# Mixed tokens of 26 tiles kept in fp32, split into fp16 halves in front of the pairs

## The chip, the cores and the metric
The kernel runs on one core of one Trainium2 chip. The metric is the device time of one execution in microseconds (us), as the median of the runs. The TensorE (PE) of this core was granted 0.989 of its full clock on average, and its full clock from 60 us on.

## The reference, cut to what matters
The input `x` has 64 batches of 64 channels of 1024 values, 4096 rows of length 1024. Two layers each add their result to `x`:

```python
# layer 0
y  = grouped_conv9(x) + ctx + bias
x1 = x + int8_product(y, W0)              # both sides rounded to int8 per row
# layer 1
x2 = einsum('boi,bih->boh', agg_w, x1) + agg_b      # the "mix"; the result is "mixed tokens"
H  = x2 @ W.T + b                          # 1024 x 1024, in fp32 accuracy
z  = x2 @ A                                # low rank, 32 columns
logits = 0.5 * H[:, anchors, :8] / max|.| + 0.5 * (z[:, anchors] @ LiMEs.T) / max|.|
p_mix  = gate(softmax(logits)) @ LiMEs
out = x1 + H + (z * p_mix) @ Bmat * scale
```

The gate needs all of `z` and the first 8 columns of `H`, so it can start only when every tile has been mixed.

## The kernel before, in words
The rows are 32 tiles of 128 (`NT = 32`). Engines work in order, each on its own list of instructions, and meet at named semaphores.

**The loop.** Turn `c` (3 to 31) of the loop on each engine does, for different tiles, the convolution of tile c (`conv`, L462, 16 fp32 calls: 8 on a column half of the array, 8 on a quarter), the mix of tile c-3 (`mix`, L505), the int8 product of tile c-2 (`int_product`, L521), some tiny transposes for row maxima (L528, L532), a transpose of the rounded tokens (`tokens_out`, L493), and in odd turns from 5 on the low rank product of the pair of tiles c-5 and c-4 (`rank_pair`, L552 and L555). After `conv` in turn c the VectorE (DVE) adds the bias (`conv_bias`, L1245), takes row maxima (L1251), the tile's scale (`tile_scale`, L1287), and evicts the two halves of the int8 product (`layer0`, L1277). `conv` itself waits, in front of its third group, for the second `layer0` of the turn before (`f_ready`).

**The mixed tile in fp16 halves.** ScalarE (ACT) reads the mixed tile from PSUM, scales it by a power of two (`t_up`) and writes the high fp16 half to a slot of the ring (`high`, L856, two instructions of 128x512). VectorE subtracts that from the PSUM value and writes the low half (`low`, L1293, two instructions of 128x512). A slot of 128 x 1024 fp32 words holds both halves. `high` waits for `t_up`.

**The low rank product.** For two tiles (256 moving columns) it multiplies the high halves with the high and low parts of the weights (104 columns, 8 matmuls, L552) and the low halves with the high weights (40 columns, alternately in the lower and the upper column half of the array, 8 matmuls, L555). `rank_out` (L1304, L1306) adds the halves for each of the two tiles.

**Two kinds of tiles.** The last six tiles (`RING = 6`, `KEPT = 26`) stay in the ring and are multiplied with W directly (`dense`, L584, 24 matmuls for each half of the columns) while the gate is computed. The 26 others go to DRAM (`save_x2`) and come back (`fetch_x2`) as 13 pairs. Each pair needs 7 products instead of 8 half-size blocks (a scheme of Strassen and Winograd; `pair`, L770, 7 x 12 matmuls of 512 columns). Its left sides are the two tiles and four sums of their halves. ACT brings both tiles to the pair's common scale (`normalized`, L902, one instruction of 128x2048 fp16 for each tile), GpSimd (POOL) adds high and low half to fp32 (`x_sums`, L1119), makes the four sums (`s_sums`, L1128), and ACT and POOL split these into fp16 halves (`s_high` L914, `s_low` L1134). The products read the tiles from the ring and the sums from homes of their own. SyncE issues the fetches in a written order; ACT issues the stores of finished tiles between its own instructions.

Of the kernel before, what the change touches and what calls it, by code (L numbers as in the profile page):

```python
# [15 lines left out]
P = 128  # L16
# [11 lines left out]
ZR = R + E  # L28
# [25 lines left out]
def program(nc, x, x_phases, conv_taps, pack, w_nat, w_rows, w_q, mix_w, w_b, b_ffn, out):  # L54
    ctx = ExitStack()
    with ctx:
# [19 lines left out]
        ring_flat = ring[:, :, :].rearrange("p s l -> p (s l)")  # L76
        x2_cols = ring_flat.bitcast(F16).rearrange("p (s h c t) -> p s h c t", s=RING, h=2, c=NL)
# [52 lines left out]
        z_w = sb("z_w", [P, NL, ZW], F16)  # L130
        z_col = sb("z_col", [P, 1], F32)
# [25 lines left out]
        z_lo = sb("z_lo", [ZR, P], F32)  # L157
# [13 lines left out]
        ratio = sb("ratio", [P, KEPT], F32)  # L171
# [66 lines left out]
        def x_sum(i):  # L238
            return (bias_b, wsum_b)[i]
# [13 lines left out]
        def _(sp):  # L253
# [55 lines left out]
            def save_x2(t):  # L309
                wait(sp, "lo_ready", 2 * t + 2)  # L310
                sp.dma_start(x2_dram[t], ring[:, t % RING, :]).then_inc(sem(f"x2_moved{t % RING}"), 16)
# [45 lines left out]
            def fetch_x2(n):  # L357
                t = ORDER[n]
                if n < 2 * RING:
                    sp.wait_ge(sem("dense_ready"), 2 * (n - RING) + 2)  # L360
                else:
                    sp.wait_ge(sem("prod_ready"), 7 * ((n - 2 * RING) // 2 + 1))
# [56 lines left out]
        def _(pe):  # L419
# [76 lines left out]
            def mix(t):  # L496
# [3 lines left out]
                wait(pe, "lo_ready", 2 * t)  # L500
# [41 lines left out]
            def rank_pair(t):  # L542
                wait(pe, "lo_ready", 2 * t + 4)
                wait(pe, "z_ready", t)
                if t == 0:
                    pe.wait_ge(sem("z_col_ready"), 1)
                if t >= NT - 4:
# [21 lines left out]
            def dense(n, h, lo=0, hi=NL):  # L569
                if lo == 0:  # L570
# [8 lines left out]
                    pe.wait_ge(sem("lo_ready"), 2 * (KEPT + n) + 2)  # L579
# [175 lines left out]
            def x2_part(n, half):  # L755
                return lambda a, k: x2_cols[:, x2_slot(n), a, 4 * half + k, :]
# [16 lines left out]
            def pair(j, deltas):  # L773
                n1, n2 = RING + 2 * j, RING + 2 * j + 1
                sum_a, sum_b, sum_c = pair_banks(j)
                pe.wait_ge(sem("norm_ready"), 2 * j + 2)
# [3 lines left out]
                product(sum_a, x2_part(n1, 0), w_part_of(0, 0), True)  # L780
# [23 lines left out]
                product(sum_c, x2_part(n1, 1), w_part_of(1, 0), True)  # L804
# [3 lines left out]
                product(sum_a, x2_part(n2, 1), t_part(1, 0), False)  # L808
# [9 lines left out]
        def _(act):  # L818
# [78 lines left out]
            def normalized(n):  # L897
                t, s = ORDER[n], x2_slot(n)
                act.wait_ge(sem(f"x2_moved{s}"), 16 * (len(range(s, KEPT, RING)) + n // RING))
                act.wait_ge(sem("ratio_ready"), 1)  # L900
                cols = x2_cols[:, s, :, :, :].rearrange("p h c t -> p (h c t)")
                A(cols, cols, ACT.Copy, scale=ratio[:, t:t + 1]).then_inc(sem("norm_ready"), 1)  # L902

            def s_high(j):
# [7 lines left out]
                for i in (1, 0):  # L912
                    act.wait_ge(sem("s_sum_ready"), 6 * j + (4 if i else 6))
                    A(s_home(j, i)[:, :, 0, :], x_sum(i)[:, :].rearrange("p (s n) -> p s n", s=2), ACT.Copy).then_inc(sem("s_hi_ready"), 1)  # L914
# [45 lines left out]
            A(z_w[:, :, R:ZR], pk[:, PACK["w8"]].rearrange("p (k r) -> p k r", k=NL), ACT.Copy, scale=s_up[:, 0:1]).then_inc(sem("rank_hi_ready"), 1)  # L960

# [47 lines left out]
            A(gateT, bank(2)[:, 0:P], ACT.Copy).then_inc(sem("gateT_ready"), 1)  # L1009
            t_high(3)  # L1010
# [17 lines left out]
            normalized(9)  # L1028
            z_high(1, 0)
# [4 lines left out]
            normalized(11)  # L1034
            store(2)
# [5 lines left out]
            for j in range(1, PAIRS):  # L1041
# [3 lines left out]
                if j + 2 < PAIRS:  # L1045
                    normalized(2 * j + 10)
                    normalized(2 * j + 11)
                store(2 * j + 5)
# [9 lines left out]
        def _(pool):  # L1058
# [52 lines left out]
            def x_sums(j):  # L1111
                for i in range(2):
                    n = RING + 2 * j + i
# [537 lines left out]
```

## Time and profile before
| | before |
|---|---|
| median of 3 runs | 648.18 us (647.95 to 648.85) |
| span of the profiled execution | 646.6 us |
| PE busy | 623.8 us, 96% |
| DVE / ACT / POOL busy | 418.3 / 335.3 / 336.2 us |
| mean DMA rate | 214 GB/s |

The span is counted from the first to the last instruction. The whole time of the profiled execution itself is not given beside it; the three timed runs lie 1.4 to 2.3 us above the span. The page draws a busy PE nearly everywhere; VectorE is at 7 to 8 tenths in the first half and at 4 in the second.

### The profile page before, as it was taken

How to read it: one execution, taken by the hardware profiler on the slowest of the kernel's cores; microseconds unless marked ns; L12 is line 12 of the kernel's file. 1: busy time of each engine (PE TensorE's matmuls, PEld its weight loads, DVE VectorE, ACT ScalarE, POOL GpSimd, SP SyncE). 2: the span in 40 equal slices, each digit the busy share in tenths (PEclk: the TensorE clock that was granted, in tenths of full speed). 3: DMA queues.
4: the chain of work that ended last, by engine and by line, in shares of the span. 5: the costliest groups of instructions: out<-in, count | busy, mean ns of one | idle time of the engine just before them, and what ended most of it. 6: DMA issues, size and time to landing. Idle time of an engine off the chain costs nothing.

```text
span 646.6 us, 14948 instructions
## 1 busy us (share of the span) xinstructions
PE 623.8 (96%) x5865; PEld 337.3 (52%) x5898; DVE 418.3 (65%) x891; ACT 335.3 (52%) x566; POOL 336.2 (52%) x223
## 2 busy tenths in 40 slices
PE   7789999999999999999999999999999999999997
PEld 5556565566566666656554444444444444444443
DVE  5958778877787778787537797745544433444434
ACT  2857898667778777776652436334333313333100
POOL 3012222217778522225485689886866678666400
PEclk8799999999999999999999999999999999999999
DMA  8969877677799797764529014554555433457103
GB/s 299 361 137 365 295 284 273 233 266 276 280 342 336 285 359 280 259 229 140 217 73 357 35 34 153 206 203 156 196 195 193 158 132 136 162 197 259 66 1 130
DMA packets 46707, 138.38 MB, mean 214 GB/s; under 512 B 13180, under 2 KB 13468, under 8 KB 46465
## 3 DMA queue, kind: packets, MB, share of 16 engines
q1 hardware_dynamic: 41886, 120.65, 52.6%
q10 hardware_dynamic: 4752, 16.78, 6.4%
q8 instruction: 47, 0.77, 0.5%
q14 instruction: 22, 0.18, 0.1%
HBM read 89.13 MB, written 48.28 MB: 213 GB/s over the span
## 4 chain that ended last, share of the span: by engine, by line
PE 51%; DVE 1%; issue 0%; ACT 0%; DVEq 0%
PE ps L770 36%; PE ps L584 9%; PE ps L752 2%; PE ps L521 2%; PE ps L505 1%; PE ps L462 0%; PE ps L552 0%; DVE z_lo L1304 0%; DVE unscale L1441 0%; DVE ring L1293 0%; DVE yb L1245 0%; DVE zT L1306 0%; PE ps L555 0%; PE ps L730 0%; PE ps L493 0%
## 5 line engine op out<-in xcount | busy, mean ns | idle before, releaser
L1088 POOL TENSOR_TENSOR x<-x_in,f_both 128x512 f32<-128x512 f32 x64 | 74.0, 1157 | 195.9 <-DVE f_both L1277 195.9
L521 PE MATMUL ps<-wqT,yq_both 128*128 128x512 bf16 x479 | 113.2, 379 | 6.0 <-issue 4.6
L462 PE MATMUL ps<-x_ph,conv_w 64*64 64x256 f32 (+1 forms) x1024 | 98.2, 396 | 2.2 <-DMA conv_w<-in_conv_taps 2.0
L863 ACT ACTIVATE yv<-yb,yinv 128x128 f32<-128x128 f32 x256 | 78.0, 389 | 2.3 <-DVE yinv L1268 2.2
L902 ACT ACTIVATE ring<-ring,ratio 128x2048 f16<-128x2048 f16 x26 | 50.6, 1994 | 51.1 <-DVE wst L1537 14.1
L770 PE MATMUL ps<-ffn_wT,ring 128*128 128x512 f16 x312 | 71.6, 379 | 0.0
L462 PEld LDWEIGHTS ps<-x_ph,conv_w 64*64 64x64 f32 (+1 forms) x1024 | 51.1, 137 | 37.4 <-issue 14.2
L521 PEld LDWEIGHTS ps<-wqT,yq_both 128*128 128x128 bf16 x512 | 45.2, 97 | 48.4 <-issue 1.0
L1245 DVE TENSOR_TENSOR yb<-ps,ybias 128x1024 f32<-128x1024 f32 x32 | 39.1, 1223 | 41.1 <-PE ps L462 41.0
L584 PE MATMUL ps<-ffn_wT,ring 128*128 128x512 f16 x288 | 64.6, 379 | 0.0
L856 ACT ACTIVATE ring<-ps,t_up 128x512 f16<-128x512 f32 x64 | 40.5, 683 | 45.5 <-issue 38.1
L1119 POOL TENSOR_TENSOR bias_b<-ring 128x1024 f32<-128x1024 f16 x13 | 27.8, 2137 | 48.4 <-ACT ring L902 48.2
L1550 DVE SCALAR_TENSOR_TENSOR x_in<-ps,unscale,x_in 128x512 f32<-128x512 f32 x30 | 22.5, 750 | 43.7 <-PE ps L770 43.5
L1277 DVE SCALAR_TENSOR_TENSOR f_both<-ps,tok_scale,wsc_b 128x512 f16<-128x512 f32 x64 | 47.8, 748 | 4.1 <-PE ps L521 3.3
L770 PEld LDWEIGHTS ps<-ffn_wT,ring 128*128 128x128 f16 x312 | 30.5, 98 | 36.8
L846 ACT ACTIVATE yq_both<-ps 128x1024 bf16<-128x1024 f16 x32 | 32.7, 1023 | 31.3 <-PE ps L493 31.0
L1293 DVE SCALAR_TENSOR_TENSOR ring<-ps,t_up,ring 128x512 f16<-128x512 f32 x64 | 46.9, 737 | 0.8 <-ACT ring L856 0.8
L584 PEld LDWEIGHTS ps<-ffn_wT,ring 128*128 128x128 f16 x288 | 27.2, 98 | 32.1 <-issue 0.8
L1550 DVE SCALAR_TENSOR_TENSOR wst<-ps,unscale,wst 128x512 f32<-128x512 f32 x28 | 21.0, 750 | 35.2 <-PE ps L770 35.1
L1251 DVE TENSOR_REDUCE rowmax<-yb 128x8 f32<-128x1024 f32 x32 | 39.0, 1220 | 1.0
L505 PEld LDWEIGHTS ps<-mixT,x 64*64 64x64 f32 x2048 | 35.8, 135 | 5.2 <-issue 1.6
L1550 DVE SCALAR_TENSOR_TENSOR x<-ps,unscale,x 128x512 f32<-128x512 f32 x21 | 15.8, 750 | 31.1 <-PE ps L770 31.1
(284 smaller groups left out, 1096.6 us busy)
## 6 DMA issues: line engine op xcount, KB each, us to landing
x_ph<-in_x_phases SPq DMA_DIRECT2D x32, 516.0 KB, 6.1
x_in<-in_x SPq DMA_DIRECT2D x32, 512.0 KB, 6.4
x_scratch<-x SPq DMA_DIRECT2D x32, 512.0 KB, 2.8
x_scratch<-ring SPq DMA_DIRECT2D x26, 512.0 KB, 4.1
ring<-x_scratch SPq DMA_DIRECT2D x26, 512.0 KB, 4.3
wst<-in_w_rows SPq DMA_DIRECT2D x12, 512.0 KB, 5.0
x_in<-x_scratch SPq DMA_DIRECT2D x12, 512.0 KB, 6.5
out<-x_in ACTq DMA_DIRECT2D x12, 512.0 KB, 3.6
```

Source lines behind the costliest of these rows:

```text
L462: return mm(ps_conv[o, g * 2 * MB:(g + 1) * 2 * MB], conv_w[k, g, w.start + o.start:w.start + o.stop], xp[k, g, :, view], start=first, sto ...
L505: last = mm(bank(2 + e)[j * 64:(j + 1) * 64, k * CH:(k + 1) * CH], x1[b, t % 2, l:l + 64], mixT[b, t, b], start=True, stop=True)
L521: last = mm(acc_bank(t, h), yqT[:, t % 2, p, :], wqT[:, p, h * HALF:(h + 1) * HALF], start=p == 0, stop=p == PH - 1)
L584: last = mm(o, x2_cols[:, x2_slot(n), a, k, :], ffn_wT[:, w, k, h * HALF:(h + 1) * HALF], start=k == 0 and i == 0, stop=k == NL - 1 and i ...
L770: last = mm(b, left(a, k), right(w, k), start=fresh and k == 0 and i == 0, stop=k == 3 and i == 2, skip_group_check=True)
L856: A(x2_cols[:, t % RING, 0, :, h * CH:(h + 1) * CH], bank(2 + h).rearrange("p (c t) -> p c t", c=NL), ACT.Copy, scale=t_up[:, t % 4:t % 4 ...
L863: last = A(yv[:, s, :], yb[:, t % 2, s, :], ACT.Copy, scale=yinv[:, s:s + 1], bias=MAGIC)
L902: A(cols, cols, ACT.Copy, scale=ratio[:, t:t + 1]).then_inc(sem("norm_ready"), 1)
L1088: g.tensor_tensor(x1[:, t % 2, s], x_in[:, t % 3, s], f16[:, s], ALU.add).then_inc(sem("x1_ready"), 1)
L1277: v.scalar_tensor_tensor(f16[:, s], acc_bank(t, h), tok_scale[:, t % 4:t % 4 + 1], wsc_b[:, s], ALU.mult, ALU.mult).then_inc(sem("f_ready" ...
L1293: v.scalar_tensor_tensor(x2_cols[:, t % RING, 1, :, cols], bank(2 + h).rearrange("p (k t) -> p k t", k=NL), t_up[:, t % 4:t % 4 + 1], x2_c ...
L1550: v.scalar_tensor_tensor(buf, src, unscale[:, t:t + 1], buf, ALU.mult, ALU.add).then_inc(sem("pair_folded"), 1)
```

## The change
For the 26 tiles that become pairs, `high` copies the mixed tile from PSUM to the ring in fp32, without a scale and without waiting for `t_up`, and `low` does nothing. The low rank product of these tiles takes fp32 operands: 8 calls of 40 weight columns, alternately in the lower and upper column half. `rank_out` is then two additions for the pair, without scales. In front of the pairs, `normalized` scales 1024 fp32 values, `x_high` (ACT) and `x_low` (POOL) write the fp16 halves of the parts of the two tiles that the products read (the whole of the first tile, the second half of the second) to one of three homes, and `s_sums` then works in place in the ring slot. `x_sums` is gone. The first product of a pair now waits for `x_low` where it waited for `normalized`; `mix` waits for `high` where it waited for `low`; the fetch of later tiles waits for `s_low` of the pair that used the slot, where it waited for all of that pair's products.

```diff
             def rank_pair(t):
-                wait(pe, "lo_ready", 2 * t + 4)
+                if t < KEPT:
+                    pe.wait_ge(sem("hi_ready"), 2 * t + 4)
...
+                if t < KEPT:
+                    for k in range(NL):
+                        o = 64 * (k % 2)
+                        last = mm(rank[o:o + ZR, 0:2 * P], z_f[:, k, :], x2_sums[:, s:s + 2, k, :],
+                                  start=k < 2, stop=k >= NL - 2, skip_group_check=True)
+                    last.then_inc(sem("z_psum"), 1)
+                    return
...
             def high(t, h):
...
-                    wait(act, "t_ready", 2 * t + 2)
+                    if t >= KEPT:
+                        act.wait_ge(sem("t_ready"), 2 * t + 2)
...
+                if t < KEPT:
+                    A(x2_sums[:, t % RING, :, h * CH:(h + 1) * CH], bank(2 + h).rearrange("p (c t) -> p c t", c=NL),
+                      ACT.Copy).then_inc(sem("hi_ready"), 1)
+                    return
...
             def normalized(n):
...
-                cols = x2_cols[:, s, :, :, :].rearrange("p h c t -> p (h c t)")
-                A(cols, cols, ACT.Copy, scale=ratio[:, t:t + 1]).then_inc(sem("norm_ready"), 1)
+                A(ring[:, s, :], ring[:, s, :], ACT.Copy, scale=pair_inv[:, t:t + 1]).then_inc(sem("norm_ready"), 1)
+
+            def x_high(j):
+                act.wait_ge(sem("norm_ready"), 2 * j + 2)
...
+                if j >= 3:
+                    act.wait_ge(sem("prod_ready"), 7 * (j - 2))
+                for i, lo in ((1, HALF), (0, 0)):
+                    A(x_home(j, i)[:, 0, lo:L], x_tile(j, i)[:, lo:L], ACT.Copy).then_inc(sem("x_hi_ready"), 1)
...
+            def x_low(j):
+                for i, lo in ((1, HALF), (0, 0)):
+                    pool.wait_ge(sem("x_hi_ready"), 2 * j + (1 if i else 2))
+                    h = x_home(j, i)
+                    g.tensor_tensor(h[:, 1, lo:L], x_tile(j, i)[:, lo:L], h[:, 0, lo:L], ALU.subtract).then_inc(sem("x_lo_ready"), 1)
...
             def low(t, h):
+                if t < KEPT:
+                    return
...
             def rank_out(t):
+                if t < KEPT:
+                    dve.wait_ge(sem("z_psum"), t // 2 + 1)
+                    dve.wait_ge(sem("z_bias_ready"), t // 8 + 1)
+                    cols = slice(t * P, (t + 2) * P)
+                    link(v.tensor_tensor(z_lo[:, :], rank_bank(t)[64:ZW, 0:2 * P], zT[64:ZW, cols], ALU.add))
+                    v.tensor_tensor(zT[0:ZR, cols], rank_bank(t)[0:ZR, 0:2 * P], z_lo[:, :], ALU.add).then_inc(sem("z_ready"), 2)
+                    return
```

Besides, two ACT instructions write the fp32 weights `z_f` once in front of the loop, the tile `ratio` goes, and the program is built with a smaller scratch area for descriptors made by software (2048 bytes); all of its large transfers use the hardware queues.

## Rows read from the trace of the kernel before
**Rows 1.** Windows: us, busy us of each engine (x instructions), clock, DMA share, GB/s.
```profile
240.00:300.00 60.00, 58.88 (x888) 36.70 (x892) 48.42 (x121) 41.94 (x93) 18.94 (x16) 1.00 0.70 247
450.00:500.00 50.00, 50.00 (x233) 22.64 (x232) 23.85 (x32) 17.32 (x12) 36.50 (x22) 1.00 0.50 184
```
**Rows 2.** Timeline of PE, 200 to 219 us: start, length, instructions.
```profile
200.92 0.62 PE L493 MATMUL ps<-identh,yv 128*128 128x128 f16 x8
201.38 1.04 PE L552 MATMUL ps<-ring,z_w 128*104 128x256 f16 x8
202.34 0.62 PE L555 MATMUL ps<-ring,z_w 128*40 128x256 f16 x8
202.79 2.92 PE L462 MATMUL ps<-x_ph,conv_w 128*64 128x256 f32 x32
205.54 1.11 PE L505 MATMUL ps<-mixT,x 64*64 64x64 f32 x64
210.27 0.22 PE L532 MATMUL ps<-ident,chanmax_rep 8*128 8x8 f32 x1
210.43 0.62 PE L493 MATMUL ps<-identh,yv 128*128 128x128 f16 x8
210.98 2.98 PE L462 MATMUL ps<-x_ph,conv_w 128*64 128x256 f32 x32
213.78 1.11 PE L505 MATMUL ps<-mixT,x 64*64 64x64 f32 x64
```
**Rows 3.** Groups by form, PE alone, 204.50 to 204.70 us: busy us, mean ns.
```profile
L462 PE MATMUL ps<-x_ph,conv_w 64*64 64x256 f32 x4 | 0.4, 427 | 0.0
L462 PE MATMUL ps<-x_ph,conv_w 128*64 128x256 f32 x2 | 0.4, 378 | 0.0
```
**Rows 4.** Groups by form, whole span: busy us, mean ns, idle before.
```profile
L1293 DVE SCALAR_TENSOR_TENSOR ring<-ps,t_up,ring 128x512 f16<-128x512 f32 x64 | 46.9, 737 | 0.8 <-ACT ring L856 0.8
L884 ACT ACTIVATE wst<-wst,w_up 128x1024 f32<-128x1024 f32 x4 | 4.5, 1138 | 0.2 <-DMA wst<-in_w_rows 0.2
L914 ACT ACTIVATE f_both<-wsum_b 128x1024 f16<-128x1024 f32 x7 | 7.4, 1057 | 35.2 <-POOL wsum_b L1128 35.2
L1134 POOL TENSOR_TENSOR wsc_b<-wsum_b,wsc_b 128x1024 f16<-128x1024 f32 x6 | 12.8, 2128 | 0.0
```
**Rows 5.** Timeline of PE, 66 to 124 us; in brackets idle before and its end.
```profile
68.59 0.18 PE L485 MATMUL ps<-x1sum,ones_b 128*128 128x1 bf16 x1 [0.37 <-ACT f_both L841]
77.46 0.81 PE L521 MATMUL ps<-wqT,yq_both 128*128 128x512 bf16 x3 [0.16 <-issue]
78.11 0.17 PE L485 MATMUL ps<-x1sum,ones_b 128*128 128x1 bf16 x1
81.63 3.31 PE L462 MATMUL ps<-x_ph,conv_w 128*64 128x256 f32 x32
103.78 0.81 PE L521 MATMUL ps<-wqT,yq_both 128*128 128x512 bf16 x3 [0.16 <-issue]
105.59 0.18 PE L485 MATMUL ps<-x1sum,ones_b 128*128 128x1 bf16 x1 [0.99 <-ACT f_both L841]
118.32 0.22 PE L532 MATMUL ps<-ident,chanmax_rep 8*128 8x8 f32 x1 [0.15 <-DVE chanmax_rep L1257]
119.03 3.19 PE L462 MATMUL ps<-x_ph,conv_w 128*64 128x256 f32 x32
```
**Rows 6.** Timelines of ACT (96 to 124 us) and DVE (72 to 86 us).
```profile
97.66 1.27 ACT L856 ACTIVATE ring<-ps,t_up 128x512 f16<-128x512 f32 x2 [1.28 <-DVE t_down L1288]
...
82.02 0.75 DVE L1277 SCALAR_TENSOR_TENSOR f_both<-ps,tok_scale,wsc_b 128x512 f16<-128x512 f32 x1
```
**Rows 7.** Timelines of POOL, 336 to 424 us, and PE, 300 to 400 us.
```profile
365.57 1.26 POOL L1104 TENSOR_TENSOR conv_w<-conv_w 128x512 f32<-128x512 f32 x1
301.77 3.30 PE L462 MATMUL ps<-x_ph,conv_w 128*64 128x256 f32 x32
...
393.17 2.75 PE L770 MATMUL ps<-ffn_wT,ring 128*128 128x512 f16 x12
```

More of the change, by code:

```diff
@@ L130, in program @@
         z_w = sb("z_w", [P, NL, ZW], F16)
+        z_f = sb("z_f", [P, NL, ZR], F32)
+        x_part = sb("x_part", [P, 2, L], F32)
         z_col = sb("z_col", [P, 1], F32)
@@ L236, in t_home, with x_home, x_tile @@
             return t_homes[q].rearrange("p (w r n) -> p w r n", w=2, r=2)
-        def x_sum(i):
-            return (bias_b, wsum_b)[i]
+        x_homes = ((x_part[:, 0, :], x_part[:, 1, :]), tuple(yb[:, i, :, :].rearrange("p n m -> p (n m)") for i in range(2)),
+                   (bias_b[:, :], wsum_b[:, :]))
+        def x_home(j, i):
+            return x_homes[j % 3][i].bitcast(F16).rearrange("p (a n) -> p a n", a=2)
+        def x_tile(j, i):
+            return ring[:, x2_slot(RING + 2 * j + i), :]
         s_homes = ((yq_both[:, :, :].rearrange("p a n -> p (a n)").bitcast(F16), f_both[:, :, :].rearrange("p a n -> p (a n)")),
@@ L499, in mix @@
                 wait(pe, "x1_ready", 2 * t + 2)
-                wait(pe, "lo_ready", 2 * t)
+                if t <= KEPT:
+                    wait(pe, "hi_ready", 2 * t)
+                else:
+                    pe.wait_ge(sem("lo_ready"), 2 * (t - KEPT))
                 for k in range(NL):
@@ L753, in delta, with x2_part @@
                 last.then_inc(sem("delta_ready"), 1)
-            def x2_part(n, half):
-                return lambda a, k: x2_cols[:, x2_slot(n), a, 4 * half + k, :]
+            def x2_part(j, i, half):
+                return lambda a, k: x_home(j, i)[:, a, (4 * half + k) * P:(4 * half + k + 1) * P]
             def s_part(j, i, s):
@@ L803, in pair @@
                 wait(pe, "pair_folded", 7 * j)
[L804 removed]
+                product(sum_c, x2_part(j, 0, 1), w_part_of(1, 0), True)
                 for n in deltas[5]:
@@ L807, in pair @@
                 pe.wait_ge(sem("pair_folded"), 7 * j + 5)
-                product(sum_a, x2_part(n2, 1), t_part(1, 0), False)
+                product(sum_a, x2_part(j, 1, 1), t_part(1, 0), False)
             dense(5, 0)
@@ L960, in _ @@
             A(z_w[:, :, R:ZR], pk[:, PACK["w8"]].rearrange("p (k r) -> p k r", k=NL), ACT.Copy, scale=s_up[:, 0:1]).then_inc(sem("rank_hi_ready"), 1)
+            A(z_f[:, :, 0:R], pk[:, PACK["a"]].rearrange("p (k r) -> p k r", k=NL), ACT.Copy, scale=s_up[:, 1:2]).then_inc(sem("z_f_ready"), 1)
+            A(z_f[:, :, R:ZR], pk[:, PACK["w8"]].rearrange("p (k r) -> p k r", k=NL), ACT.Copy, scale=s_up[:, 0:1]).then_inc(sem("z_f_ready"), 1)
             for c in range(3, NT):
@@ L1009, in _ @@
             A(gateT, bank(2)[:, 0:P], ACT.Copy).then_inc(sem("gateT_ready"), 1)
+            x_high(0)
             t_high(3)
@@ L1028, in _ @@
             normalized(9)
+            x_high(1)
             z_high(1, 0)
@@ L1034, in _ @@
             normalized(11)
+            x_high(2)
             store(2)
@@ L1047, in _ @@
                     normalized(2 * j + 11)
+                    x_high(j + 2)
                 store(2 * j + 5)
@@ L1151, in _ @@
             t_sums(3)
-            x_sums(0)
+            x_low(0)
             t_low(3)
@@ L1156, in _ @@
             for j in range(1, PAIRS):
-                x_sums(j)
+                x_low(j)
                 s_sums(j)
```

54 lines of the change are left out of this document (25 added, 29 removed).

## The prediction
> **What bounds the kernel now.** I read the table of windows first. PE is busy for 58.9 of 60 us late in the loop and for 50.0 of 50 in the pairs, at the full clock throughout [rows 1]. So nearly every microsecond that PE's instruction list gains or loses is a microsecond of the time, and what the other engines gain counts only where PE waits for them. A busy figure overlaps pipelined matmuls, so I then took the timeline of PE and measured from start to start. A turn of the loop from one conv to the next is 8.19 us without a low rank product (210.98 less 202.79). The reader is to see two things there: PE goes from one piece to the next without a pause, and the only regular gap is one of 0.16 us behind the mix [rows 2, 5]. Last I looked for turns that are longer than their kind, since there another engine bounds: there are six that matter, all listed below.
>
> **PE: the low rank product.** Before: from the first L552 to the conv behind it, 202.79 - 201.38 = 1.41 us [rows 2]. After: 8 calls in fp32. What such a call costs, conv shows: its 16 calls make 32 instructions, so a call is two, and the first 16 of them (the 8 calls on a column half, 256 columns, all 128 rows, the same shape as the new ones) run from 202.79 to about 204.50, where the first quarter-array instruction stands beside the last half-array ones [rows 2, 3]. That is 1.71 us for 8 calls with both halves at work. The new product has 8 calls of that shape, with 40 weight columns where conv has 64: 1.71 us. There is one more item: the eight transposes in front take 201.38 - 200.92 = 0.46 us when the low rank product follows on the whole array, and 210.98 - 210.43 = 0.55 us when conv follows on column halves [rows 2]; the new product begins on a half, so it pays 0.09. Behind it comes conv, on halves already, as it did behind L555, so nothing changes there. A pair of tiles costs 1.71 + 0.09 - 1.41 = 0.39 us more. All 13 pairs of the kept tiles stand in the loop (turns 5 to 29); the pairs 26, 28 and 30 keep the old form. 13 x 0.39 = 5.1 us. Bounds: 4.6 if the 0.09 does not show and the weight loads of 40 columns help a little, 6.2 if the alternation costs another 0.08 each time.
>
> The Trainium skill (FP8 and Floating Point Precision, on true FP32) says that such a product is four passes through the array; this trace agrees, with two instructions of two passes each. It is the rule that speaks against the change: 8 calls x 4 passes on half the array are 16 full passes of 256 columns, where the fp16 form had 8 full and 8 half ones, 12. By the rule alone the pair would cost a third more than 1.28 us, 0.43, and 13 pairs 5.5. TensorEngine Tiling, Key Properties (Trainium skill) says that changing the tiling mode drains the array; the 0.09 above would be that drain, and the two rows agree.
>
> **VectorE and ACT in the loop.** `low` goes for 26 tiles: 52 x 737 ns = 38 us of VectorE [rows 4]. PE bounds the loop, so most of this buys nothing. Two waits move earlier, though. (a) The second `layer0` of a turn stands behind the first `low`, so its result comes 0.73 us earlier, and conv's third group waits for it. In turn 7 that `layer0` ends at 82.02 + 0.75 = 82.77, while conv began at 81.63 and wants it about 0.85 later (half of the half-array stage of 1.71); this conv lasts 3.31 us instead of 2.98 [rows 2, 5, 6]. (b) ACT's `high` no longer waits for `t_up`. In turn 8 ACT stood idle for 1.28 us in front of `high`, which began at 97.66 [rows 6]; two extra copies behind it then made everything late, and in turn 9 the row total on PE came 105.59 - 103.78 = 1.81 us behind the int8 product instead of 78.11 - 77.46 = 0.65 [rows 5].
> What this gives back, turn by turn: turn 5, the row total waited with 0.37 us idle [rows 5] and 0.15 more hidden under the matmul in front, 0.5; turn 7, 0.33; turn 9, 1.81 - 0.65 = 1.16; turn 10, where VectorE was late with the channel maxima (0.15 idle [rows 5], the rest hidden), 0.4; turn 11, conv 3.19 us instead of 2.98 [rows 2, 5] and a wait of 0.18 for a scale, 0.4; turn 31, conv 3.30 us [rows 7], 0.3. Together 3.1. Then there is a trifle that repeats: conv takes 2.80 us behind transposes (213.78 - 210.98) but 2.75 behind a low rank product (205.54 - 202.79) [rows 2], where `layer0` had been done long before. If that 0.05 is the same wait, it goes in 9 turns, 0.4. I take half of it: 3.3 us back. Bounds 0 (the waits are replaced by others of equal length) and 4.0.
> `high` writing fp32 costs what it did: ACT's 1024-element copies take 1138 ns to fp32 and 1057 to fp16 [rows 4], under 0.1 us an instruction, and ACT has time to spare in each turn. Bound: 0 to 0.3 us in all. The two writes of `z_f` stand behind ACT's third rounding of tokens, in front of the first row sums; estimated from the two like them that are there, under 1 us of ACT, and PE reads these sums later than that: 0 to 0.5 us, taken as 0. `rank_out` becomes two instructions of twice the width instead of four, off the path.
>
> **The pairs.** PE's 7 x 12 matmuls and the deltas are unchanged and leave no gap, so only lateness can cost. ACT for a pair: before 2 x 1994 ns of `normalized`; after 2 x 1138 and 1057 + about 600 for `x_high`, 3.9 us against 4.0 [rows 4]. POOL: before 2.1 + 2.3 us of `x_sums`; after 2128 ns and about 1270 for half of it [rows 4], 1.0 us less. The new condition is that the first product waits for `x_low`. For pair 0: POOL is through with the sums in front of it at 366.8, `x_high` is done before, so `x_low` ends at about 370.2; PE wants it at 393.2 [rows 7]. Cover 23 us. Later pairs are prepared two ahead, 38 us of PE work, against some 20 us of ACT and POOL. The fetches wait for something earlier than before, so SyncE's queue does not hold them longer. Cost 0; bound, if the cover went, a few tenths for each pair.
>
> **The sum.** The profiled span is 646.6 us; what lies around it (1.6 to the median of 648.18) does not change. 648.2 + 5.1 - 3.3 = 650.0 us. Without the return it is 653.3.
>
> **Rivals.**
> 1. *The pass cost stands alone* (the waits in turns 5 to 11 only change hands: ACT and VectorE are in order, and the two copies and the delta weights are still there). For it: VectorE had unexplained pauses in turn 7. Against: the idle of ACT in front of `high` is plain. 653.3 us. Chance 0.2.
> 2. *Not slower*: the PE step that turns the maxima back (L532) waits for VectorE in every turn. It begins at 210.27 and the transposes 0.16 later [rows 2], where the product in front of it should be through 0.1 us earlier. If a VectorE with 1.5 us less work in a turn brings the maxima sooner, 26 turns give 2.6 us more: 647.4. Against: the maxima hang on conv, bias and `layer0`, none of which stands behind `low` in that chain. It decides if those maxima come 0.1 us earlier. Chance 0.13.
> 3. *The halves don't run together in fp32 at 40 columns*: 16 instructions of 0.213 us in a row, 3.4 us, 13 x 1.7 = 22 us more, about 672. Against: conv does it. Chance 0.04.
> 4. *The pairs wait*, through `x_low` or the homes that are reused three pairs later: say 0.5 us for each, 13 x 0.5 = 6.5, 656.5. Chance 0.05.
>
> **How the numbers follow.** The forecast, 650.0, has 0.58; its own range is 648.8 to 651.6. The whole range is 647.5 to 653.8: it takes in rivals 1 and 2 and leaves out 3, 4 and a little. What a measurement of this kernel can tell from no change is 0.2%, 1.3 us, so "within" is 646.9 to 649.5. The forecast's case is slower by over that with about 0.65 of its weight, rivals 1, 3, 4 wholly; rival 2 is mostly within. Faster by over 0.2% is left 0.06.
>
> **What would show it.** L552 and L555 are left in three pairs only; 16 fp32 instructions for each of 13 pairs in 1.7 us, and 0.55 us of transposes in front of them. A turn with a low rank product longer by 0.39, one without unchanged or 0.05 shorter. The row total of turn 9 at 0.65 behind the product, conv at 2.75 to 2.8 us in turns 7, 10 and 31. PE without a gap from the first pair on. The prediction is wrong if the fp32 product takes another time than 1.7 us, if the excess of turns 5 to 11 stays, or if any pair begins late.

## The result and the profile after

The change makes the kernel slower: 650.71 us (median of 5 runs, 650.49 to 651.80) against 648.18 us (647.53 to 648.85), ratio 1.0044 [1.0031, 1.0056]. The profiled execution has a span of 649.7 us where the one of before had 646.6.

The busy figures say that all other engines lost work. This is the first part of the page of the kernel after:

```profile
PE 634.5 (98%) x5898; PEld 336.7 (52%) x5898; DVE 374.7 (58%) x812; ACT 327.6 (50%) x594; POOL 322.2 (50%) x223
```

VectorE lost 43.6 us of work, ACT 8 and POOL 14, and PE is drawn busy for 98% of the span where it was 96% (mostly records that the trace of before lacks, see below). The windows late in the loop and in the pairs (us, busy us of each engine in the order PE, PEld, DVE, ACT, POOL, clock, DMA share, GB/s) answer to [rows 1]:

```profile
240.00:300.00 60.00, 60.00 (x861) 35.51 (x861) 37.91 (x100) 41.99 (x97) 17.42 (x15) 1.00 0.70 249
450.00:500.00 50.00, 50.00 (x233) 22.64 (x232) 23.13 (x31) 15.54 (x16) 34.50 (x22) 1.00 0.48 167
```

PE is full in both, at its full clock (2.4 GHz). In the pairs it runs the same 233 instructions as before, so the pairs give and take nothing. In the loop VectorE went from 48.4 to 37.9 us of 60, and PE has no free time that this could give back. The timeline of PE after, 200 to 224 us (start, length, instructions), beside [rows 2]:

```profile
201.65 0.62 PE L501 MATMUL ps<-identh,yv 128*128 128x128 f16 x8
202.20 1.93 PE L569 MATMUL ps<-ring,z_f 128*40 128x256 f32 x16
203.96 2.93 PE L470 MATMUL ps<-x_ph,conv_w 128*64 128x256 f32 x32
206.71 1.11 PE L516 MATMUL ps<-mixT,x 64*64 64x64 f32 x64
...
211.60 0.62 PE L501 MATMUL ps<-identh,yv 128*128 128x128 f16 x8
212.15 2.98 PE L470 MATMUL ps<-x_ph,conv_w 128*64 128x256 f32 x32
214.95 1.11 PE L516 MATMUL ps<-mixT,x 64*64 64x64 f32 x64
```

From start to start: the transposes 0.55 us in front of the new product as in front of conv (they were 0.46 in front of the old one), the new product 203.96 - 202.20 = 1.76 us where the old one took 1.41. The turn without a product is still 8.19 us (212.15 - 203.96), conv behind the transposes still 2.80.

All turns of the loop, from the start of one conv to the start of the next, in us:

| turn | before | after | after less before | given back (0.43 less that, in turns with a product) |
|---|---|---|---|---|
| 5 | 10.11 | 10.00 | -0.11 | 0.54 |
| 7 | 9.90 | 10.00 | +0.10 | 0.33 |
| 9 | 10.73 | 10.00 | -0.73 | 1.16 |
| 10 | 8.58 | 8.19 | -0.39 | 0.39 (no product) |
| 11 | 10.25 | 10.44 | +0.19 | 0.24 |
| 13 | 10.18 | 10.57 | +0.39 | 0.04 |
| 15 to 25, 29 | 9.90 | 10.33 | +0.43 | 0 |
| 27 | 10.20 | 10.64 | +0.44 | 0 |
| 4, 6, 8, 12 to 30 even | 8.18 to 8.76 | the same to 0.01 | 0 | 0 |
| 31 and the dense part | 91.40 | 91.08 | -0.32 | 0.32 (no product) |

(From turn 15 on an odd turn also holds two small products for the gate, so 9.90 is its kind there and 9.57 in turns 5 to 9.) The last line runs from the conv of turn 31 to the first product of a pair (301.77 to 393.17, and 305.12 to 396.20). So 13 x 0.43 = 5.6 us were added and 3.0 were given back: +2.6 us. The measured medians differ by 2.5. The two spans differ by 3.1, and 0.4 of it stands in front of turn 5, where the start of the kernel puts conv at 63.34 or 63.74; in all the profiles taken here conv of turn 4 begins anywhere between 54.15 and 55.70 us, and in the two profiles of this same kernel at 55.43 and 54.93, so the start is scatter.

### The profile page after: what moved, and what is told of

It reads as the page before. It is cut to its first block, busy times and chain, and to the rows that moved or that the text cites. A ratio compares the mean times of both kernels' runs of the same rounds, so it can differ in the third digit from the quotient of the medians.

```text
span 649.7 us, 14865 instructions
## 1 busy us (share of the span) xinstructions
PE 634.5 (98%) x5898; PEld 336.7 (52%) x5898; DVE 374.7 (58%) x812; ACT 327.6 (50%) x594; POOL 322.2 (50%) x223
## 4 chain that ended last, share of the span: by engine, by line
PE 79%; DVE 1%; issue 0%; ACT 0%; DVEq 0%
PE ps L792 36%; PE ps L532 12%; PE ps L606 9%; PE ps L470 9%; PE ps L516 3%; PE ps L569 3%; PE ps L774 2%; PE ps L501 2%; PE ps L589 1%; PE ps L543 0%; PE ps L539 0%; PE ps L574 0%; DVE unscale L1487 0%; DVE z_lo L1351 0%; DVE ring L1333 0%
## 5 line engine op out<-in xcount | busy, mean ns | idle before, releaser
L532 PE MATMUL ps<-wqT,yq_both 128*128 128x512 bf16 x512 | 120.5, 379 | 0.8 <-ACT wsc_b L849 0.8
L470 PE MATMUL ps<-x_ph,conv_w 64*64 64x256 f32 (+1 forms) x1024 | 96.6, 390 | 0.0
L532 PEld LDWEIGHTS ps<-wqT,yq_both 128*128 128x128 bf16 x512 | 45.2, 97 | 48.2 <-issue 0.9
L1166 POOL TENSOR_TENSOR ring<-ring 128x512 f32<-128x512 f32 x52 | 66.0, 1268 | 4.0
L606 PE MATMUL ps<-ffn_wT,ring 128*128 128x512 f16 x288 | 64.6, 379 | 0.0
L927 ACT ACTIVATE ring<-ring,pair_inv 128x1024 f32<-128x1024 f32 x26 | 28.4, 1140 | 54.4 <-DVE x_ph L1583 14.4
L606 PEld LDWEIGHTS ps<-ffn_wT,ring 128*128 128x128 f16 x288 | 27.2, 98 | 32.1 <-issue 0.8
L516 PE MATMUL ps<-mixT,x 64*64 64x64 f32 x2048 | 35.6, 218 | 0.0
L862 ACT ACTIVATE f_both<-x 128x1024 bf16<-128x1024 f32 x32 | 33.4, 1043 | 0.0
L879 ACT ACTIVATE ring<-ps 128x512 f32<-128x512 f32 x52 | 27.8, 585 | 2.6 <-PE ps L516 2.3
L792 PE MATMUL ps<-ffn_wT,x_part 128*128 128x512 f16 x120 | 27.5, 379 | 0.0
```

Of the source, the lines that this page charges most:

```text
L470: return mm(ps_conv[o, g * 2 * MB:(g + 1) * 2 * MB], conv_w[k, g, w.start + o.start:w.start + o.stop], xp[k, g, :, view], start=first, sto ...
L516: last = mm(bank(2 + e)[j * 64:(j + 1) * 64, k * CH:(k + 1) * CH], x1[b, t % 2, l:l + 64], mixT[b, t, b], start=True, stop=True)
L532: last = mm(acc_bank(t, h), yqT[:, t % 2, p, :], wqT[:, p, h * HALF:(h + 1) * HALF], start=p == 0, stop=p == PH - 1)
L606: last = mm(o, x2_cols[:, x2_slot(n), a, k, :], ffn_wT[:, w, k, h * HALF:(h + 1) * HALF], start=k == 0 and i == 0, stop=k == NL - 1 and i ...
L792: last = mm(b, left(a, k), right(w, k), start=fresh and k == 0 and i == 0, stop=k == 3 and i == 2, skip_group_check=True)
L1166: g.tensor_tensor(o, x, y, op).then_inc(sem("s_sum_ready"), 1)
```

## The experiments

Each run is compared with the kernel before on the same chip; what matters more is its difference from the kernel after, for which there is a second measurement at the end: 650.67 us. The turn lengths are taken from the trace as above.

### The price of the product: the product twice

```diff
-                    for k in range(NL):
+                    for k in list(range(NL)) + list(range(NL)):
                         o = 64 * (k % 2)
                         last = mm(rank[o:o + ZR, 0:2 * P], z_f[:, k, :], x2_sums[:, s:s + 2, k, :],
```

> The changed kernel with the fp32 low rank product of each of the 13 pairs done twice over, the second time on top of the first from the start. Theory A (PE bounds the loop and a product costs its 16 instructions at 0.107 us, 1.71 to 1.76 us): 13 x 1.71 = 22.2 us more, 672.9. Rival B (part of the product lies under waits): clearly less than 22 us more.

Measured: 673.15 us (672.66 to 674.36), ratio 1.0382 [1.0364, 1.0400], so 22.4 us above the kernel after. PE in this kernel, 212 to 219 us:

```profile
213.03 3.65 PE L569 MATMUL ps<-ring,z_f 128*40 128x256 f32 x32
216.51 2.93 PE L470 MATMUL ps<-x_ph,conv_w 128*64 128x256 f32 x32
```

32 instructions take 216.51 - 213.03 = 3.48 us, twice 1.76 less the 0.04 that the second pass saves at its start; 13 x 1.72 = 22.4, all of what was measured. It follows that each microsecond of this product counts in full: nothing lies beside it. What the old product cost (1.41 us, and 0.09 less in the transposes) was not doubled; it is read from the trace, but the 0.43 us between the two stands in the length of seven turns in which PE's list differs in nothing else, 9.90 against 10.33 us. The 0.04 is worth a second look: the product costs 1.76 us behind the transposes and 1.72 behind work on halves.

### Does the alternation of the column halves matter

```diff
-                    for k in range(NL):
+                    for n, k in enumerate((0, 2, 4, 6, 1, 3, 5, 7)):
                         o = 64 * (k % 2)
```

(The four calls on the lower half first, then the four on the upper; the same calls.)

> The changed kernel with the 8 calls of the low rank product ordered by column half, four for the lower and then four for the upper, instead of alternating. Theory A (the price of 1.76 us needs both halves at work at once; instructions on one half run one after another): 16 x 0.213 = 3.4 us a pair, 13 x 1.65 = 21.5 us more, 672. Rival B (the array takes 0.107 us for such an instruction anyway): no change, 650.7.

Measured: 663.04 us (662.47 to 663.60, 2 runs), ratio 1.0220 [1.0198, 1.0242]: 12.3 us above the kernel after. PE, 109 to 116 us:

```profile
109.56 2.17 PE L569 MATMUL ps<-ring,z_f 128*40 128x256 f32 x13
111.36 0.43 PE L470 MATMUL ps<-x_ph,conv_w 128*64 128x256 f32 x1
111.57 0.38 PE L569 MATMUL ps<-ring,z_f 128*40 128x256 f32 x1
...
112.00 0.38 PE L569 MATMUL ps<-ring,z_f 128*40 128x256 f32 x1
112.06 3.08 PE L470 MATMUL ps<-x_ph,conv_w 128*64 128x256 f32 x29
114.96 1.11 PE L516 MATMUL ps<-mixT,x 64*64 64x64 f32 x64
```

The product is not over when conv begins at 111.36: the last instructions of its upper half alternate with the first ones of conv on the lower half. Nor are its own halves one behind the other. The first row below is a piece of PE's timeline from the start of the upper half on; then come windows of 0.1 us with this product alone (busy of PE, instructions in the window), then the same in the kernel after, and the product's last two instructions there:

```profile
110.46 0.63 PE L569 MATMUL ps<-ring,z_f 128*40 128x256 f32 x3
```

```profile
110.30:110.40 0.10, 0.10 (x2) 0.05 (x1) 1.00 0.80 328
110.90:111.00 0.10, 0.10 (x4) 0.10 (x2) 1.00 0.80 328
```

```profile
202.90:203.00 0.10, 0.10 (x4) 0.10 (x2) 1.00 0.92 369
...
203.74 0.39 PE L569 MATMUL ps<-ring,z_f 128*40 128x256 f32 x2
```

At first two instructions are in flight, those of the lower half; from 110.46 on there are four, as in the alternating product (the row does not name the half; that the new ones are the upper half's is read from the starts, 0.21 to 0.22 us apart on a half), though three of the eight instructions of the lower half are still to start (13 of the 16 have started when conv begins). So the upper half starts 0.90 us late and ends as much late. The turn with the product grows by 0.04 us and the turn that this conv opens from 8.19 to 9.04, together 0.89 x 13 = 11.6 of the 12.3 us. The forecast for a serial product (some 21.5 us) is missed because the upper half starts while the lower one is still at work. What conv does on the free lower half gains nothing: from the last start of the product (112.00) to the mix (114.96) it is 2.96 us, in the kernel after from 203.74 to 206.71 it is 2.97. So the two halves do run together in fp32 with 40 columns, and it is the alternation that gets this from the first instruction on.

### ACT waits for `t_up` again

```diff
-                    if t >= KEPT:
-                        act.wait_ge(sem("t_ready"), 2 * t + 2)
+                    act.wait_ge(sem("t_ready"), 2 * t + 2)
```

> The changed kernel with one wait put back: ScalarE's first half of `high` waits for the tile's scale in all tiles, as before. Theory A (the waits of turns 5 and 9 in the old kernel came from this wait, and their going gave 0.54 + 1.16 = 1.7 us back): these two turns grow again to 10.5 and 11.1 us from 10.00, span +1.7, about 652.4. Rival B (the row totals are in time now because a turn with the low rank product is 0.43 us longer and leaves slack): both turns stay at 10.0, time as the changed kernel, 650.7.

Measured: 652.33 us (651.88 to 653.00), ratio 1.0061 [1.0046, 1.0076]. Turn 5 is 10.36 us (+0.36 on the kernel after), turn 7 10.10 (+0.10), turn 9 10.98 (+0.98), every other turn as after: +1.44. First ACT in turn 8 of this kernel, then PE's row totals in turns 5 and 9 (in brackets the idle time and what ended it):

```profile
98.52 1.08 ACT L878 ACTIVATE ring<-ps 128x512 f32<-128x512 f32 x2 [2.00 <-DVE t_down L1325]
```

```profile
68.81 0.18 PE L493 MATMUL ps<-x1sum,ones_b 128*128 128x1 bf16 x1 [0.19 <-ACT f_both L862]
106.27 0.18 PE L493 MATMUL ps<-x1sum,ones_b 128*128 128x1 bf16 x1 [0.81 <-ACT f_both L862]
```

In the kernel after, the same copy and the same total:

```profile
95.96 1.06 ACT L879 ACTIVATE ring<-ps 128x512 f32<-128x512 f32 x2
```

```profile
104.84 0.17 PE L493 MATMUL ps<-x1sum,ones_b 128*128 128x1 bf16 x1
```

One wait of ACT that hangs on VectorE brings back the chain of [rows 6]: ACT idle for 2.00 us in front of `high`, the copies behind it late, the row sums late, PE idle for 0.81 us. This one wait is worth 0.36 of the 0.54 us given back in turn 5 and 0.98 of the 1.16 in turn 9, 1.34 of the 3.0 in all. The 0.10 of turn 7 is not a part of them: here it stands in front of the row total, while the 0.33 that turn 7 had before stood inside conv.

### VectorE gets its instruction back

```diff
                 if t < KEPT:
+                    dve.wait_ge(sem("t_ready"), 2 * t + 2)
...
+                    v.scalar_tensor_tensor(junk, bank(2 + h).rearrange("p (k t) -> p k t", k=NL), t_up[:, t % 4:t % 4 + 1],
+                                           x2_sums[:, t % RING, :, cols], ALU.mult, ALU.subtract).then_inc(sem("junk_ready"), 1)
                     return
...
                 if t <= KEPT:
                     wait(pe, "hi_ready", 2 * t)
+                    wait(pe, "junk_ready", 2 * t)
```

(The second place is `mix` on PE. The instruction is of the shape of `low` and writes to `x_part`, which nothing reads before the pairs write it anew.)

> The changed kernel with VectorE's work put back: for each half of the 26 tiles it reads the PSUM bank and the ring slot and writes a 128x512 fp16 result to a spare place, where `low` stood, and the mix waits for it as it did. The extra work is not part of the result. Theory A: the waits that hung on VectorE come back in turns 7, 10, 11 and 31 (0.33 + 0.39 + 0.24 + 0.32 = 1.3 us), about 652.0; conv in turn 7 takes 3.1 instead of 2.80 us. Rival B (VectorE's work was under PE throughout, and its late results were pauses of other cause): no change, 650.7.

Measured: 651.35 us (650.84 to 652.09), ratio 1.0047 [1.0030, 1.0065], 0.6 above the kernel after. Turns 5 to 10 are as after, to 0.02 us, and turn 11 is 10.46; turn 13 is longer by 0.05. Only conv in turn 31 is at 3.31 us, as it was before. Its line on PE and the one on VectorE inside it:

```profile
304.38 3.31 PE L470 MATMUL ps<-x_ph,conv_w 128*64 128x256 f32 x32
```

```profile
304.64 0.20 DVE L1307 RECIPROCAL yinv<-yscale 128x8 f32<-128x8 f32 x1 [0.44 <-issue]
```

38 us of VectorE put back cost 0.07 us in turns 11 and 13, and the intervals of the two kernels overlap. The 0.33 us of turn 31 is not the put-back work: this edit puts nothing into turn 31, whose `low` is that of tile 28, one of the last six, and stands in all these kernels. What is new there is that VectorE stood still for 0.44 us. The theory that VectorE's load made turns 7, 10 and 11 long falls for this kernel.

### Both, and then the third edit too

`both_back` has the two edits above. `all_back` has them and also `rank_out` as four instructions of 128 columns instead of two of 256:

```diff
-                    link(v.tensor_tensor(z_lo[:, :], rank_bank(t)[64:ZW, 0:2 * P], zT[64:ZW, cols], ALU.add))
-                    v.tensor_tensor(zT[0:ZR, cols], rank_bank(t)[0:ZR, 0:2 * P], z_lo[:, :], ALU.add).then_inc(sem("z_ready"), 2)
+                    for i in range(2):
+                        cols = slice((t + i) * P, (t + i + 1) * P)
+                        link(v.tensor_tensor(z_lo[:, 0:P], rank_bank(t)[64:ZW, i * P:(i + 1) * P], zT[64:ZW, cols], ALU.add))
+                        v.tensor_tensor(zT[0:ZR, cols], rank_bank(t)[0:ZR, i * P:(i + 1) * P], z_lo[:, 0:P], ALU.add).then_inc(sem("z_ready"), 1)
```

> Both of these together, so only the low rank product, the writes of the fp32 weights and the pairs differ from the old kernel. Theory A: all 3.0 us of the return are gone; 650.7 + 3.0 = 653.7, which is 648.2 + 13 x 0.43 + about 0.8 for the weights at the start less 0.9 of differences in the start. Rival B: 650.7 to 651.5.

> As `both_back`, and `rank_out` again in four instructions of 128 columns instead of two of 256. Read from the profile only: turn 10, which took 8.58 us in the old kernel and 8.20 with both put back. Theory A2 (in turn 10 of the old kernel VectorE had its share of B and then four instructions of `rank_out` in front of conv's bias; the two wide ones save about 0.7 us there, and the longer product gives PE's side 0.43 us more): the bias starts some 0.3 us late, turn 10 at 8.2 to 8.4. Rival B2 (`rank_out` plays no part): 8.20 exactly as in `both_back`.

Measured: `both_back` 652.96 us (650.70 to 653.25), ratio 1.0062 [1.0041, 1.0083]; `all_back` 653.0 us in its one run. `both_back` has turn 5 at 10.37, 7 at 10.10, 9 at 10.98, 10 at 8.20, 13 at 10.62, and conv of turn 31 at 3.31 us: the turns show the two edits simply added, 1.44 + 0.05 + 0.33 = 1.8 us (the median is 2.2 us above that of the kernel after, among runs that spread over 2.6). Both forecasts are missed: of the 3.0 us given back, some 1.2 did not return. VectorE of `both_back` in turn 31, and then PE:

```profile
305.52 0.73 DVE L1338 SCALAR_TENSOR_TENSOR ring<-ps,t_up,ring 128x512 f16<-128x512 f32 x1
...
306.85 0.20 DVE L1306 RECIPROCAL yinv<-yscale 128x8 f32<-128x8 f32 x1 [0.44 <-issue]
306.98 0.75 DVE L1315 SCALAR_TENSOR_TENSOR f_both<-ps,tok_scale,wsc_b 128x512 f16<-128x512 f32 x1
```

```profile
306.59 3.31 PE L470 MATMUL ps<-x_ph,conv_w 128*64 128x256 f32 x32
```

Here is the price of the pause: VectorE stands still for 0.44 us with nothing to wait for, the second `layer0` behind it ends at 307.73, 1.14 after conv began, and conv, which wants it after about 0.85, loses 0.33. In the kernel before it is the same picture in turn 7, and in turn 31 too:

```profile
81.89 0.20 DVE L1268 RECIPROCAL yinv<-yscale 128x8 f32<-128x8 f32 x1 [0.45 <-issue]
...
302.15 0.75 DVE L1277 SCALAR_TENSOR_TENSOR f_both<-ps,tok_scale,wsc_b 128x512 f16<-128x512 f32 x1 [0.28 <-issue]
```

In the kernel after the one pause falls into turn 29, where it costs nothing. Its turn 31 has the same `low` in front of the second `layer0` as before, and no pause; this `layer0` ends at 305.91, 0.79 us after conv began, just in time, and conv is at 2.98 us as in turn 7:

```profile
295.55 0.75 DVE L1315 SCALAR_TENSOR_TENSOR f_both<-ps,tok_scale,wsc_b 128x512 f16<-128x512 f32 x1 [0.28 <-issue]
...
304.06 0.73 DVE L1333 SCALAR_TENSOR_TENSOR ring<-ps,t_up,ring 128x512 f16<-128x512 f32 x1
...
305.16 0.75 DVE L1315 SCALAR_TENSOR_TENSOR f_both<-ps,tok_scale,wsc_b 128x512 f16<-128x512 f32 x1
```

```profile
81.93 2.98 PE L470 MATMUL ps<-x_ph,conv_w 128*64 128x256 f32 x32
...
305.12 2.98 PE L470 MATMUL ps<-x_ph,conv_w 128*64 128x256 f32 x32
```

So the excess of turns 7 and 31 is this: with `low` in front of it, `layer0` is only just in time, and a pause that falls there costs 0.33 us. In turn 31 the change took nothing away but the pause's place; in turn 7 it took away both, and `low` put back without a pause costs nothing there (`dve_back`, `both_back`). Whether a pause alone would, no run shows. `all_back` has a second way to be late, without a pause: in turn 7 its `low` waits 0.16 us for ACT's `high`, `layer0` ends 1.03 us after conv began, and the turn is 10.22 us.

In `all_back` turn 10 is 8.19 us: the 0.39 us of turn 10 in the kernel before could not be brought back by any of the three edits. What is left of the differences (the old product and the scaled `rank_out`, ACT's slower fp16 copy) was not put back one by one. The cause of turn 10's 0.39 stays open, and so do 0.18 in each of turns 5 and 9 and the 0.24 of turn 11: about 1.0 us of the 3.0. Turn 4 (+0.22) and turn 11 (+0.39) of `all_back` are longer than in the kernel after; the one of turn 11 has such a pause in it too (125.70, 0.25 us).

### The `z_f` writes

```diff
-            A(z_f[:, :, 0:R], pk[:, PACK["a"]].rearrange("p (k r) -> p k r", k=NL), ACT.Copy, scale=s_up[:, 1:2]).then_inc(sem("z_f_ready"), 1)
-            A(z_f[:, :, R:ZR], pk[:, PACK["w8"]].rearrange("p (k r) -> p k r", k=NL), ACT.Copy, scale=s_up[:, 0:1]).then_inc(sem("z_f_ready"), 1)
...
+                if c == 3:
+                    A(z_f[:, :, 0:R], pk[:, PACK["a"]].rearrange("p (k r) -> p k r", k=NL), ACT.Copy, scale=s_up[:, 1:2]).then_inc(sem("z_f_ready"), 1)
+                if c == 4:
+                    A(z_f[:, :, R:ZR], pk[:, PACK["w8"]].rearrange("p (k r) -> p k r", k=NL), ACT.Copy, scale=s_up[:, 0:1]).then_inc(sem("z_f_ready"), 1)
                 tokens_sb(c - 1)
```

> The changed kernel with ScalarE's two writes of the fp32 low rank weights moved from in front of the loop into turns 3 and 4, into the time in which ScalarE waits for the transposes. Theory A (these writes made the first row sums late: in turn 3 the row total stands 1.65 us behind the product in front of it, where 0.87 is usual): turn 3 shorter by 0.8 us, 649.9. Rival B (the row total of turn 3 is late for another reason, the first transfers and the low clock at the start): no change, 650.7.

Measured: 650.86 us (649.15 to 652.76, 10 runs), ratio 1.0040 [1.0025, 1.0054]: no change. But the trace shows why one has to look further than one wait. PE in turn 3, first the kernel after, then this one:

```profile
51.25 0.18 PE L493 MATMUL ps<-x1sum,ones_b 128*128 128x1 bf16 x1 [0.62 <-ACT f_both L862]
...
52.90 0.27 PE L539 MATMUL ps<-ident,rowmax 128*8 128x128 f32 x1
```

```profile
50.46 0.18 PE L493 MATMUL ps<-x1sum,ones_b 128*128 128x1 bf16 x1
...
52.74 0.27 PE L539 MATMUL ps<-ident,rowmax 128*8 128x128 f32 x1 [0.57 <-DVE bound L1321]
```

The row total waited 0.62 us for ACT, and the writes were a cause of it; without them this idle is gone, and 0.57 us appear in front of the next step, which waits for VectorE. Turn 3 is 9.67 us in both. The writes cost nothing because another wait of the same length stands behind theirs.

### The cover of the pairs

```diff
-                    g.tensor_tensor(h[:, 1, lo:L], x_tile(j, i)[:, lo:L], h[:, 0, lo:L], ALU.subtract).then_inc(sem("x_lo_ready"), 1)
+                    for n in range(2):
+                        last = g.tensor_tensor(h[:, 1, lo:L], x_tile(j, i)[:, lo:L], h[:, 0, lo:L], ALU.subtract)
...
+                    last.then_inc(sem("x_lo_ready"), 1)
```

> The changed kernel with GpSimd's `x_low` done twice for each part, about 3.4 us more of GpSimd for each pair. Theory A (the new wait of the pairs' first product has 20 us and more of cover): no change, PE without a gap, 650.7. Rival B (the pairs stand close to GpSimd): up to 13 x 3.4 us more.

Measured: 651.70 us (649.40 to 652.10), ratio 1.0042 [1.0025, 1.0060], the ratio of the kernel after. The window 450 to 500 us:

```profile
450.00:500.00 50.00, 50.00 (x233) 22.61 (x232) 22.93 (x31) 16.51 (x18) 45.48 (x28) 1.00 0.49 175
```

POOL goes from 34.5 to 45.5 us of 50 and PE still does its 233 instructions. In the kernel after `x_low` of the first pair ends 369.83 + 3.25 = 373.08 us, and PE takes it at 396.20 (POOL, then PE):

```profile
369.83 3.25 POOL L1157 TENSOR_TENSOR x_part<-ring,x_part 128x512 f16<-128x512 f32 x2
```

```profile
396.20 2.75 PE L792 MATMUL ps<-ffn_wT,x_part 128*128 128x512 f16 x12
```

### The gains without the price: the kernel before, smoothed

If what the change gave back are late waits in turns 5 to 11 and pauses that meet no slack, the kernel before can have that by order alone, without the fp32 product.

```diff
-                if 4 <= c < 8:
-                    z_bias(c - 4)
-                if c == 8:
+                if c in (5, 11, 12, 14):
+                    z_bias((5, 11, 12, 14).index(c))
+                if c == 13:
                     act.wait_ge(sem("b_loaded"), 16)
...
-                if c == 9:
+                if c == 14:
                     delta_weights()
...
                 low(c - 3, 0)
-                scales(c)
                 layer0(c - 2, 1)
+                scales(c)
                 low(c - 3, 1)
```

`before_smooth2` differs in turn 11 alone, where the order is `scales`, `layer0`, `low`, `low`.

> The old kernel, its arithmetic untouched, with the work of the long turns moved: the four scalings of z's bias from turns 4 to 7 to turns 5, 11, 12 and 14, the two copies of B from turn 8 to 13, VectorE's share of B from turn 9 to 14, and the second `layer0` of a turn in front of the tile scales. Theory A (the waits that the change took away can be had without the fp32 product): turn 5 0.5, turn 7 0.3, turn 9 1.2, turn 10 0.4, turn 31 0.3 us shorter, 2.5 to 3 us less than before, 645.5. Rival B (the late pieces come back in the turns to which they are moved): 648.2.

> As `before_smooth`, but in turn 11 VectorE makes the tile scales ahead of the second `layer0`, since there PE waits for them in front of a transpose (1.46 us in front of it instead of 0.81 in the old kernel). Theory A: turn 11 shorter by 0.6 to 0.9 us, 644.6 us. Rival B (that transpose waits for the running maximum of W's row sums): no change, 645.4.

Measured: 645.36 us (643.99 to 646.75), ratio 0.9948 [0.9927, 0.9968], and 645.10 us (644.70 to 646.43), ratio 0.9946 [0.9928, 0.9964]. Turns 5, 7 and 9 are 9.57, 9.57 and 9.56 us in the first, turn 10 is 8.19. Turn 4 of the second is 8.84 us (8.31 in the first), in a start that scatters. Turn 11 is 10.71, because the first weight bound (L679) now waits for a `scales` that had moved behind; in the second it is 10.04, 0.67 shorter as forecast, of which the median shows 0.26. The line of `before_smooth`, then that of `before_smooth2`:

```profile
126.42 0.27 PE L679 MATMUL ps<-ident,w_max 128*1 128x128 f32 x1 [0.84 <-DVE yinv L1268]
```

```profile
125.52 0.27 PE L679 MATMUL ps<-ident,w_max 128*1 128x128 f32 x1 [0.17 <-DVE yinv L1268]
...
81.53 2.98 PE L462 MATMUL ps<-x_ph,conv_w 128*64 128x256 f32 x32
...
104.00 0.17 PE L485 MATMUL ps<-x1sum,ones_b 128*128 128x1 bf16 x1
```

The row total of turn 9, which had 0.99 us of idle [rows 5], has none, and conv of turn 7 is at 2.98. `before_smooth2` beats both kernels, by 3.2 us the one before and by 5.6 us the one after, and does the same arithmetic as the kernel before. The two moves (ACT's and VectorE's pieces to later turns, `layer0` ahead of the tile scales) were not run apart; 0.66 us of the gain is turns 7 and 31, which also have no pause in front of `layer0` here. The same order in the kernel after wasn't run; its turns 5 to 10 have nothing left to give back.

### The kernel after once more

> The changed kernel again, on the same chip as the kernel before and the smoothed one, for the size of the difference. Theory A (13 x 0.43 = 5.6 us for the product, 2.7 to 3.0 back): 648.2 + 2.6 to 2.9, a ratio of 1.0040 to 1.0045. Rival B (the profiled spans, 3.1 us apart, are the better measure): 1.0048.

Measured: 650.67 us (649.51 to 652.03, 10 runs), ratio 1.0034 [1.0022, 1.0046], 2.4 us. Its median is that of the first measurement to 0.04 us. The ratio lies just below the forecast from the turns (1.0040 to 1.0045), which its interval holds; the 1.0048 of the spans is outside. Its turns without a product are 8.19 us again, though its trace draws a 0.16 us gap in them that the first profile of this kernel did not have (below).

## Why the prediction came out as it did

The forecast was 650.0 us, the result 650.7. The balance is the one that it named, a price on PE of which a part is given back where other engines had been late, and the price is shown. Of the return less than half came for the reason given; that its sum came out nearly right is in part luck. Step by step:

- **PE bounds, and its list is the time.** Right. 22.4 us more in the list made 22.4 us more in the time; 38 us more on VectorE made 0.07 in the turns that have them (0.6 in the median, with the pause of turn 31).
- **The product: 0.39 us for a pair, 5.1 in all.** Right in kind, small in size: this is the mis-sized term. It measured 0.43 and 5.6. The mode change was right to the row (0.55 us of transposes, +0.09, in each of the 13 turns). The 1.71 us, read off inside conv [rows 3], is right for 16 instructions that follow work on halves (1.72 in `rank_twice`); what is missing is 0.04 for the start behind the transposes, where it takes 1.76. The rows had it: conv too takes 2.80 us behind transposes and 2.75 behind a product, and the prediction put that 0.05 down as a wait. The pass count of the Trainium skill (FP8 and Floating Point Precision, on true FP32), which the prediction set beside its own sum as an estimate of 0.43 for a pair and 5.5 in all, comes to the measured 0.43 and 5.6, but not by its own terms: the product alone took 0.35 more (1.76 - 1.41), and the rest is the 0.09 in front.
- **The waits given back: 3.3 us.** 3.0 measured. Turns 5, 7, 9, 10 and 31 gave 0.54, 0.33, 1.16, 0.39 and 0.32, as listed (0.5, 0.33, 1.16, 0.4, 0.3); turn 11 gave 0.24 instead of 0.4. The reason (b), ACT no longer waits for `t_up`, is shown for 1.34 us, in turns 5 and 9. The reason (a), `low` in front of the second `layer0`, is not borne out: in turn 31 `low` stands there in both kernels, and in turn 7 it did nothing when put back. Both turns had a pause of VectorE before. The 0.32 of turn 31 came back because in the kernel after the pause falls elsewhere, the 0.33 of turn 7 for that or because `low` no longer takes the slack, which no run separates. The prediction knew of such pauses (rival 1) but gave them no term. With the pause in turn 31, as in `dve_back`, 0.33 less is given back. Turn 10's 0.39 came as predicted, but not for the reason given: none of the three edits brought it back. Its cause is open, as are 0.18 us in each of turns 5 and 9 and the 0.24 of turn 11.
- **The 0.05 us of conv behind transposes.** Did not go; conv is at 2.80 there as before. It is no wait, so the 0.2 taken for it was wrong. That it has to do with the change from the whole array to halves is likely, as it stands behind transposes alone and the new product pays 0.04 there as well (1.76 against 1.72), but no run took it apart.
- **A regular gap of 0.16 us behind the mix.** There is none. It was a record missing from the trace. The rows of the page for the int8 product, before and after:

```profile
L521 PE MATMUL ps<-wqT,yq_both 128*128 128x512 bf16 x479 | 113.2, 379 | 6.0 <-issue 4.6
```

```profile
L532 PE MATMUL ps<-wqT,yq_both 128*128 128x512 bf16 x512 | 120.5, 379 | 0.8 <-ACT wsc_b L849 0.8
```

  479 of 512 matmuls were recorded before, all 512 after; "idle" falls from 6.0 to 0.8 us and the turn stays at 8.19. The prediction put nothing into its sum for this gap, so it cost nothing but a false picture; the PE share of 96% before and 98% after is largely that.
- **`high` in fp32 at no cost.** Better than that. The three groups, ACT after, ACT before for `high`:

```profile
L879 ACT ACTIVATE ring<-ps 128x512 f32<-128x512 f32 x52 | 27.8, 585 | 2.6 <-PE ps L516 2.3
L927 ACT ACTIVATE ring<-ring,pair_inv 128x1024 f32<-128x1024 f32 x26 | 28.4, 1140 | 54.4 <-DVE x_ph L1583 14.4 <-DVE wst L1583 14.3 <-DVE x_in L1583 13.2
```

```profile
L856 ACT ACTIVATE ring<-ps,t_up 128x512 f16<-128x512 f32 x64 | 40.5, 683 | 45.5 <-issue 38.1 <-DVE t_down L1288 4.3 <-PE ps L505 3.1
```

  585 ns instead of 683. Off the path, it shows nowhere in the time. `normalized` at 1140 ns is the 1138 of [rows 4].
- **`z_f` at no cost.** Right in the sum, for a reason that was not given: PE did wait for ACT there (0.62 us), but a wait of the same length stood behind it.
- **The pairs at no cost.** Right: cover 23.1 us where 23 was predicted, and with `x_low` twice still no gap.

Of the rivals, the first (nothing given back, 653.3) falls with turns 5 to 10, though what it had for it, the pauses, is what made turns 7 and 31 long; the second (L532 sooner in every turn, 647.4) with the 8.19 us that did not move; the third (the halves do not run together) with 1.76 us for 16 instructions; the fourth with the windows of the pairs.

## What to carry to other kernels

When PE is full, price a change by the start-to-start time of PE's pieces alone: 38 us of VectorE's work were worth almost nothing, 0.43 us in each of 13 turns of PE's own list cost 5.6. Turns that are longer than their kind are where other engines count; look there for a wait that can be moved by order alone, before paying for it with arithmetic, since that gave 3.2 us without the price. Before an instruction is blamed for such a turn, look whether it is still there in the kernel that is faster: turn 31 kept its `low` and got shorter all the same. And test an edit that removes a wait by the length of the turn, not by the idle in front of one instruction: the next wait may already stand behind it.

## What the runs showed of the hardware

- An fp32 product with 128 rows, 40 weight columns and 256 moving columns takes 0.110 us for an instruction (1.76 / 16), with instructions alternating between column halves, and 0.107 (1.72 / 16) behind other work on halves. Grouped by half, the first instruction of the second half starts 0.90 us in, beside the last four of the first half, and the loss is 0.89 us for a product.
- Behind 50 us, VectorE stands still for 0.25 to 0.45 us with nothing that it waits for: twice in the profile of before, not at all in `before_smooth`, once in each other. In all seven profiles of kernels with VectorE's program as in the kernel after (both of that kernel, `act_wait`, `zf_late`, `rank_twice`, `no_alternation`, `x_low_twice`) it stands in front of the same instruction, the second `layer0` of turn 29, though that comes anywhere from 294.27 to 315.01 us. So its place goes with VectorE's list and not with the time; where that list was edited it moved (304.64, 306.85 and 125.70 us). It costs PE 0.33 us where there is no slack. What it is stays open.
- A copy from PSUM on ACT to fp32 without a scale takes 585 ns for 128x512, one to fp16 with a scale 683; which of the two differences counts was not run.
